# Masked maxima whose mask is written into the PSUM banks by ScalarE, over three pairs of banks, and two low parts of the query moved to later rounds on VectorE

## What is computed

```python
query = _layernorm(q @ Wq + bq, qn_scale, qn_bias)
key = _layernorm(kv @ Wk + bk, kn_scale, kn_bias)
value = _layernorm(kv @ Wv + bv, vn_scale, vn_bias)
...
scores = jnp.einsum('bhqd,bhkd->bhqk', query, key) / jnp.sqrt(jnp.asarray(D_K, query.dtype))
m = mask[:, None, :, :]
scores = jnp.where(m == 0, NEG_INF, scores)
probs = jax.nn.softmax(scores, axis=-1)
out = jnp.einsum('bhqk,bhkd->bhqd', probs, value)
out = out.transpose(0, 2, 1, 3).reshape(bs, -1, D_MODEL)
return out @ Wo + bo
```

## Time and profile before

| what | value |
|---|---|
| median of 3 executions | 2463.45 us |
| the profiled execution's own time | 2461.2 us |
| its span in the trace | 2459.4 us |
| TensorE (matmul) busy | 2396.7 us, 97% |
| VectorE busy | 1503.3 us, 61% |
| ScalarE busy | 1106.3 us, 45% |
| GpSimd busy | 242.1 us, 10% |
| mask matmuls (L1429) | 256 |
| reductions (L983) | 256, 128 of them in the second layer |

### The profile page before, as it was taken

The page is one execution under the profiler, slowest core; times in us unless marked ns, Lnnn a source line. Parts: engine busy times, 40 slices in busy tenths (PEclk is TensorE's granted clock), DMA queues, the critical chain, the costliest instruction groups (busy, mean ns, idle before and its releaser), DMA issues.

```text
span 2459.4 us, 32226 instructions
## 1 busy us (share of the span) xinstructions
PE 2396.7 (97%) x12832; PEld 1822.9 (74%) x12832; DVE 1503.3 (61%) x2482; ACT 1106.3 (45%) x1794; POOL 242.1 (10%) x223
## 2 busy tenths in 40 slices
PE   7999999999999999999988999999999999999998
PEld 5666667688888888888755666666778888888886
DVE  5555566542212222223588777776888888888986
ACT  4343433442222222223344444445666666666665
POOL 1021112210000000000311111113000000000000
PEclk9999999999999999999999999999999999999999
DMA  3121112421101101101311111122400101001100
GB/s 127 35 86 52 52 52 69 159 86 52 41 12 52 52 8 45 52 18 69 118 62 49 66 66 66 66 70 91 154 18 35 52 18 52 35 29 41 35 33 19
DMA packets 89141, 140.92 MB, mean 57 GB/s; under 512 B 5024, under 2 KB 27936, under 8 KB 88992
## 3 DMA queue, kind: packets, MB, share of 16 engines
q1 hardware_dynamic: 88992, 138.87, 16.5%
HBM read 105.30 MB, written 33.55 MB: 56 GB/s over the span
## 4 chain that ended last, share of the span: by engine, by line
PE 38%; DVE 9%; ACT 2%; issue 1%; DMA 0%; POOL 0%; SPq 0%; DVEq 0%; ACTq 0%
PE l_lay_bank L69 18%; PE l_lay_score L69 11%; PE l_lay_score L1429 1%; PE l_lay_score L1431 1%; PE l_lay_values L1503 1%; DVE l_at_at_next L1048 1%; PE l_lay_sums L1515 1%; PE l_lay_values L1507 1%; DVE l_at_h_lo L1062 1%; DVE l_at_at_next L1041 1%; PE l_lay_score L1486 1%; DVE l_at_full L1037 1%; DVE l_at_full L1030 1%; DVE l_at_xTf_lo L936 1%; DVE l_at_qn L966 1%
## 5 line engine op out<-in xcount | busy, mean ns | idle before, releaser
L69 PE MATMUL l_lay_score<-l_at_tw_hi,l_at_h_hi 128*128 128x512 f32 x1024 | 401.5, 392 | 5.2 <-DVE l_at_h_lo L1062 4.7
L69 PE MATMUL l_lay_bank<-l_at_xTf_hi,l_at_tw_hi 128*128 128x512 f32 x1024 | 400.0, 391 | 0.0
L69 PE MATMUL l_lay_score<-l_at_tw_hi,l_at_h_lo 128*128 128x512 f32 x1024 | 398.8, 389 | 0.0
L69 PE MATMUL l_lay_bank<-l_at_xTf_hi,l_at_tw_lo 128*128 128x512 f32 x1024 | 398.4, 389 | 0.0
L69 PE MATMUL l_lay_bank<-l_at_xTf_lo,l_at_tw_hi 128*128 128x512 f32 x1024 | 398.4, 389 | 0.0
L69 PE MATMUL l_lay_score<-l_at_tw_lo,l_at_h_hi 128*128 128x512 f32 x1024 | 398.4, 389 | 0.0
L1022 DVE TENSOR_TENSOR l_at_h_lo<-l_at_full,l_at_h_hi 128x512 fp32r<-128x512 f32 x128 | 99.3, 777 | 466.0 <-ACT l_at_h_hi L736 466.0
L731 ACT ACTIVATE l_at_full<-l_lay_bank,l_at_lay_b 128x512 f32<-128x512 f32 x128 | 88.3, 690 | 457.6 <-PE l_lay_bank L69 457.6
L69 PEld LDWEIGHTS l_lay_score<-l_at_tw_hi,l_at_h_hi 128*128 128x128 f32 x1024 | 192.2, 188 | 49.2 <-DVE l_at_h_lo L1062 10.3
L983 DVE TENSOR_REDUCE l_at_maxes<-l_lay_score 128x4 f32<-128x616 f32 x256 | 199.9, 797 | 46.5 <-PE l_lay_score L1431 43.7
L69 PEld LDWEIGHTS l_lay_score<-l_at_tw_hi,l_at_h_lo 128*128 128x128 f32 x1024 | 192.2, 188 | 40.4
(11 more groups left out here) (224 smaller groups left out, 4133.4 us busy)
## 6 DMA issues: line engine op xcount, KB each, us to landing
both_x_in<-stream SPq DMA_DIRECT2D x25, 1024.0 KB, 5.6
l_at_xg<-stream SPq DMA_DIRECT2D x23, 1024.0 KB, 5.5
stream<-l_at_xg SPq DMA_DIRECT2D x22, 1024.0 KB, 4.3
l_at_tw_raw<-in_l_w SPq DMA_DIRECT2D x64, 256.0 KB, 5.9
both_x_in<-in_x SPq DMA_DIRECT2D x9, 1024.0 KB, 7.5
l_at_xg<-in_x SPq DMA_DIRECT2D x7, 1024.0 KB, 5.4
out<-l_at_xg SPq DMA_DIRECT2D x7, 1024.0 KB, 4.3
l_at_maskT_in<-in_maskT SPq DMA_DIRECT2D x16, 256.0 KB, 3.5
```

What stands on the lines that cost most here:

```text
L69: done = nc.tensor.matmul(out, lhs[a], rhs[b], start=first and n == 0, stop=last and n == len(passes) - 1)
```

## The change

Four things change, in the second layer alone and only for chunks 1 to 7:

1. `score`, `values` and `sums` become one tensor of six banks. Rounds 0 to 3 keep the two pairs of before; rounds 4 to 15 (`SEED0 = 4`) rotate over three pairs, the third of which is `values` and `sums`: round 4 takes the third pair, round 5 the first, round 6 the second, and so on.
2. For rounds 4 to 15 the mask matmuls are gone. ScalarE writes the mask into both banks of the pair (`seed_max`, one instruction of 128 x 616 elements with a bf16 source in which the 154 values are repeated four times), and TensorE's two key matmuls accumulate onto it. TensorE waits for that write (`seeded`); the write waits for VectorE's reduction of three rounds before (`max_done`), for round 4 for the evictions of `values` and `sums` instead.
3. On ScalarE both evictions into `q_raw` for parts 2 and 3 come first, then the eviction of the sums, then the twelve mask writes; the roundings of parts 2 and 3 stand behind the second and the third mask write.
4. On VectorE the low parts 2 and 3 come after rounds 6 and 9 in place of 2 and 3.

```diff
@@ -288,9 +288,8 @@
         bank = [n.ps(f"bank{i}", [P, 512]) for i in range(2)]
-        score = n.ps("score", [P, GH, 512])
-        values = n.ps("values", [P, 512])
-        sums = n.ps("sums", [P, 512])
+        score = n.ps("score", [P, GH + 2, 512])
+        values, sums = score[:, GH, :], score[:, GH + 1, :]
         hid, tr = bank, [values, sums]
@@ -313,6 +312,7 @@
         mask_done, maskT_done = n.sem("mask_done"), n.sem("maskT_done")
+        seeded = n.sem("seeded")
         dve_seeded, act_seeded = n.sem("dve_seeded"), n.sem("act_seeded")
@@ -344,6 +344,11 @@
         n_zero = 9 if norm else 4
+        SEED0 = 4
+        N_SEED = NM - SEED0
+        pair_of = lambda it, m: m % 2 if it == 0 or m < SEED0 else (m - 2) % 3
+        pair_before = lambda m: m - 3 if m > SEED0 else None
+        max_banks = lambda it, m: score[:, 2 * pair_of(it, m):2 * pair_of(it, m) + 2, 0:2 * KEYS]
         own_rows = [slice(DH * j, DH * (j + 1)) for j in range(GH)]
@@ -662,15 +667,31 @@
 
+            def q_raw_norm(it, t):
+                act.wait_ge(qT_ps, KT * it + t + 1)
+                nc.scalar.activation(q_raw[:, t, :], bank[t % 2][:, :], ACT.Identity,
+                                     scale=q_col[:, 0, t:t + 1], bias=q_col[:, 1, t:t + 1])\
+                    .then_inc(q_filled, 1)
+
+            def q_hi_norm(it, t):
+                act.wait_ge(q_filled, KT * it + t + 1)
+                nc.scalar.activation(qT1[0][:, t, :], q_raw[:, t, :], ACT.Copy).then_inc(q_hi, 1)
+
             def q_front_norm(it, ts):
                 for t in ts:
-                    act.wait_ge(qT_ps, KT * it + t + 1)
-                    nc.scalar.activation(q_raw[:, t, :], bank[t % 2][:, :], ACT.Identity,
-                                         scale=q_col[:, 0, t:t + 1], bias=q_col[:, 1, t:t + 1])\
-                        .then_inc(q_filled, 1)
-                    act.wait_ge(q_filled, KT * it + t + 1)
-                    nc.scalar.activation(qT1[0][:, t, :], q_raw[:, t, :], ACT.Copy)\
-                        .then_inc(q_hi, 1)
+                    q_raw_norm(it, t)
+                    q_hi_norm(it, t)
+
+            def seed_max(it, m):
+                if m == SEED0:
+                    act.wait_ge(mask_done, it + 1)
+                    act.wait_ge(c_out, KT * it)
+                    act.wait_ge(s_out, it)
+                else:
+                    act.wait_ge(max_done, NM * it + pair_before(m) + 1)
+                nc.scalar.activation(max_banks(it, m).rearrange("p a (h k) -> p a h k", h=2),
+                                     mask_add[:, m % QT, :].unsqueeze(1).unsqueeze(1)
+                                     .broadcast_to([P, 2, 2, KEYS]), ACT.Copy).then_inc(seeded, 1)
 
@@ -831,8 +852,14 @@
                 if more and norm:
-                    q_front_norm(it + 1, (2, 3))
+                    q_raw_norm(it + 1, 2)
+                    q_raw_norm(it + 1, 3)
                 s_evict(it)
+                if more and norm:
+                    for m in range(SEED0, NM):
+                        seed_max(it + 1, m)
+                        if m in (SEED0 + 1, SEED0 + 2):
+                            q_hi_norm(it + 1, m - SEED0 + 1)
                 if it == last - 1:
@@ -977,8 +1004,7 @@
                 dve.wait_ge(max_ps, NM * it + m + 1)
-                heads = score[:, 2 * (m % 2):2 * (m % 2) + 2, 0:2 * KEYS]\
-                    .rearrange("p a (h k) -> p a h k", h=2)
+                heads = max_banks(it if norm else 0, m).rearrange("p a (h k) -> p a h k", h=2)
                 to = maxes[:, q, :].rearrange("p (j c) -> p j c", c=DH)[:, :, t]
@@ -1222,8 +1248,8 @@
                     max_of(it + 1, m)
-                    if m in (2, 3) and norm:
-                        qT_front(it + 1, (m,))
+                    if m in (6, 9) and norm:
+                        qT_front(it + 1, (m // 3,))
                     if it and m in (7, 11, 14):
@@ -1411,11 +1437,14 @@
                 t, q, b = m // QT, m % QT, it // CPB
+                seed = norm and it > 0 and m >= SEED0
                 if m == 0 and norm:
                     pe.wait_ge(q_hi, KT * it + t + 1)
-                if m >= 2:
+                if seed:
+                    pe.wait_ge(seeded, N_SEED * (it - 1) + m - SEED0 + 1)
+                elif m >= 2:
                     pe.wait_ge(max_done, NM * it + m - 1)
@@ -1424,13 +1453,13 @@
                 for a in range(2):
-                    to = score[:, 2 * (m % 2) + a, 0:2 * KEYS].rearrange("p (h k) -> p h k", h=2)
-                    if norm:
+                    to = max_banks(it if norm else 0, m)[:, a, :].rearrange("p (h k) -> p h k", h=2)
+                    if norm and not seed:
                         nc.tensor.matmul(to, ident_bf[:, :], mask_add[:, q, :].unsqueeze(1)
                                             keys.bd[:, b, t, 2 * a:2 * a + 2, :],
-                                            start=not norm, stop=True)
+                                            start=not norm, stop=True, skip_group_check=seed)
                 done.then_inc(max_ps, 1)
```

## The result

Four executions of the changed kernel took 2441.20 to 2442.36 us, median 2441.83; four of the kernel before, taken beside them, 2461.83 to 2465.78, median 2462.68. The ratio is 0.9912 (95% interval 0.9898 to 0.9926): the kernel is faster by 0.9%, 20.9 us. The forecast was 2446.6 us (16.8 us less), its range 2441 to 2455. The measured time lies 0.8 us inside the lower end of that range, and outside 2443 to 2451, the part of it that the forecast held at 63 in 100. The direction and the main mechanism hold (TensorE is the bound and gets its mask matmuls back); the gain is 4 us larger than the sum gave. The profiled execution took 2441.2 us with a span of 2439.4, against 2461.2 and 2459.4 before, so the two traces differ by 20.0 us and can account for nearly all of it.

A forecast was written before the change was run, and what follows sets the result against it. TensorE was taken as the bound: a chunk of 2 to 7 gives 3.46 - 0.55 - 0.1 = 2.8 us, six give 16.8, chunk 1 gives 0, so 2446.6 us; range 2441 to 2455.

The forecast's parts named there:

- The bound and part 1: TensorE sets the pace in chunks 2 to 7; dropping mask matmuls saves 0.288 us a round, 20.7 us in six chunks.
- The rival of the exposed weight load: TensorE's second key weight load shows, 0.05 us a round stays, six chunks give some 14 us: 2449; 8 in 100.
- Part 2, the mask write: ScalarE's write of 616 elements takes 0.69 us, bounds 0.60 and 1.20, and ScalarE has room for twelve a chunk.
- The late start: ScalarE's write for round 7 ends after the shorter rounds want it, costing 0 to 0.25 us a chunk, taken as 0.1.
- Part 3, VectorE: Rounds 4 to 15: VectorE needs 12.6 us against TensorE's 11.8, so its growing lateness reaches TensorE.
- the 0.87 us of the third pair: Slack for VectorE's lateness: the mask stands 2.07 us after a round's start and is wanted after three rounds, 2.94.
- 0.55 us a chunk: TensorE's loss in rounds 4 to 15 from waits on late VectorE, with 0.1 us for each restart.
- VectorE is not slowed and TensorE gets everything: Rival: the gain is 20.7 us and a little in chunk 1, giving 2442 us; 8 in 100.
- The ends: After round 15, VectorE's last reduction is done 0.7 us before TensorE's 2.8 us of remaining work ends, so no wait.
- The low parts: Moving VectorE's low parts 2 and 3 behind later rounds costs nothing, since they are not read until after round 15.
- Part 4, chunk 1: VectorE sets the pace without an output product; gain 0, bounds 0.5 us gained and 1.0 us lost.
- a ring of 2.1 us: Chunk 1: reduction, mask write, handovers and matmuls of a pair take 2.1 us per three rounds, less than three reductions.

The follow-up runs named there:

- the second profile: The changed kernel run and profiled again without an edit: 2442.00 us, 0.9911 of the kernel before.
- The filler: Changed kernel plus two extra 512-column TensorE matmuls, results never read, after each of rounds 4 to 15 of chunk 1: 2441.30 us, ratio 0.9913.

## Why the prediction was right, and what was mis-sized

*The bound and part 1.* Right. Rounds are 0.980 us apart where 0.981 was read from the first layer, and chunks 2 to 7 give 3.4 us each, 20.4 in all (- 3.4, - 3.4 and, for chunks 4 to 7, 13.6), of the 20.7 foretold. The rival of the exposed weight load is out: two key matmuls take 0.28 to 0.30 us in the chain, not 0.33. The rule of the Trainium skill that was weighed there (TensorE: Matmul & The Clock Gate, Back-to-back issue gap) may hold as it stands, but the extra 0.05 us that I had worked out from it is not in this trace.

*Part 2, the mask write.* Foretold 0.69 us, measured 0.681 in the mean of 84. The first two, which wait for nothing, start 1.29 - 0.69 = 0.60 us apart. The Trainium skill's formula (ScalarE: Activation LUTs, What ACT_TABLE_LOAD costs) gave an estimate of 0.70, and the trace agrees. Two banks and a repeated source cost nothing extra. The late start, 0.1 us a chunk, did not come. The writes for rounds 4 and 5 run together from 1414.42 to 1415.71, so the first is done near 1415.1, and round 4 starts at 1415.34 without a wait. The working feared for the write for round 7, since it added up whole durations; in the trace writes and roundings overlap a little, that write starts at 1417.30, is done by 1417.99, and round 7 wants it at 1418.27.

*Part 3, VectorE.* This is the term that was mis-sized. The working took "2.35 / 3 = 0.783 us" for a reduction in a queue, from three reductions in the earlier trace rows. That 2.35 us ends with the whole 0.80 us of the last one, so it is not three distances but two and a duration; and in the first layer VectorE, 0.4 us late at the first of the three, had caught up by the third, which waited for TensorE. A queued reduction costs 0.70 us. The trace of before has it too, in chunk 3, where two reductions find their input ready, (1.50 - 0.80) / 1 = 0.70:

```profile
1414.46 1.50 DVE L983 TENSOR_REDUCE l_at_maxes<-l_lay_score 128x4 f32<-128x616 f32 x2
```

With it the needs of part 3 become 12 x 0.70 + 3 x 0.66 + 2 x 0.60 = 11.6 us, less than TensorE's 11.8 instead of more. The same recursion with 0.28 us of slack a round in place of 0.20 reads: 0.60 - 0.28 = 0.32 late at round 7, 0.70 at 8, 0.74 at 10, 0.84 at 12, 0.66 at 15. The trace has the reduction of round 7 at 1419.10, 0.83 after its round and so 0.35 late. The largest lateness, 0.84 at round 12 by this sum, would just fit into the 0.87 us of the third pair. In the trace it is 0.92 (the reduction starts at 1424.56, 1.40 after its round at 1423.16), so the mask for round 15 is there 1.40 + 0.80 + 0.02 + 0.69 + 0.05 = 2.96 us after round 12 where it is wanted after 2.94, and that is where the single restart of 0.1 us stands. So of "0.55 us a chunk" 0.1 came. The rival "VectorE is not slowed and TensorE gets everything", held at 8 in 100, gave the time that was measured (2442), but only half of it is what happened: VectorE is late, within what the third pair allows, and the little that the rival added for chunk 1 came out as a loss. The run without any masks confirms it from the other side: 0.1 us a chunk is left to gain.

*The ends.* Right: the transposes of the maxima never wait on the last reduction in chunks 2 to 7 (no idle time stands ahead of them in any of the six), and the stretch between round 15 and the next chunk does not grow.

*The low parts.* "Free in itself" holds in the changed kernel, but the prediction did not say what the old place would have cost: 2.9 us a chunk, since the roundings that they need now stand among the mask writes.

*Part 4, chunk 1.* Taken at 0 with bounds of - 0.5 and + 1.0; measured + 0.6, or + 0.5 by the second profile. "Chunk 1 unchanged" was among the signs, and it did not hold. The reason given for 0, a ring of 2.1 us against three reductions of 2.35, fails by the same term as part 3: three queued reductions take 2.1. The bound "if the later low parts meet a late first write" names something that the trace has: TensorE waits 1.36 us for the first write (its row is in the last section), and VectorE, which did its low parts in that time before, is idle:

```profile
1299.92 1.51 DVE L1009 TENSOR_REDUCE l_at_maxes<-l_lay_score 128x4 f32<-128x616 f32 x2 [0.94 <-PE l_lay_score L1460]
```

The granted clock has a share too. The filler, which keeps it at 1.00 and leaves this idle time as it is, gives back 0.3 us of the 0.6. And without any masks or mask writes chunk 1 still takes 53.9; what that run shares with the changed kernel is a TensorE with less to do and a granted clock of 0.55 from 1303 to 1314 us. How the 0.6 us divides between the two is not shown further.

*The sum.* 6 x 3.4 less 0.6 is 19.8 us between the first and the last transposes, against 16.8 forecast. Two terms were too dear (0.45 us a chunk in part 3, 0.1 in part 2, 3.3 in six chunks), and chunk 1 was 0.6 too cheap; the errors partly cancel, and the range held because it reached down to the whole of TensorE's share. The remaining difference of the medians, 20.9 against 20.0 in the traces, is within the scatter of the runs.

## What to carry to other kernels

Take the cost of an instruction in a queue from the distance between starts in a stretch where that engine is truly behind, not from a group's duration divided by its count; 0.08 us an instruction turned an engine that keeps up into one that does not. Work that is taken off the bounding engine pays in full only if its new owner's whole ring (reduce, write, handovers) fits into the rounds for which the buffer is free, so check ring and number of buffers together, and check what else stands behind the moved work on its engine. And look at the granted clock where the relieved engine was not the bound: chunk 1 lost there, if only 0.3 us.
